# Layer 1's attention on one core: softmax weights turned by a product with diag(1/sum), head outputs added up turned in one PSUM bank, values as the stationary operand

## The chip, the cores and the metric

One core of one Trainium2 chip runs the whole program: nine stages, one after the other, in one launch. The metric is device time in microseconds (us). Three timed runs of the kernel before took 13870.17, 13870.44 and 13876.11 us, median 13870.44. Engines are named as in the profile: PE is TensorE's matmul, PEld its load of a stationary operand ("weights"), DVE is VectorE, ACT is ScalarE, POOL is GpSimd, SP is SyncE.

## The reference, cut to what matters

The program chains a windowed token mixer and four layers of attention and feed-forward over `h`, 32 samples of 242 tokens and 64 channels. The change is within layer 1's attention, `h = h + attn(layernorm(h))`:

```
q = _rmsnorm(_rope(x @ wq.T as 16 heads of 64), q_norm_w)     # per head
k = _rmsnorm(_rope(x @ wk.T), k_norm_w);  v = x @ wv.T         # one key/value head for all 16
mask = (cols <= rows) & (rows - cols <= 128)
scores = where(mask, q @ k.T * 64**-0.5, -1e30)
attn = softmax(scores, axis=-1)
out = (attn @ v, heads side by side) @ wo.T
```

## The kernel before, in words

`stage_l1_attn` handles 32 samples x 16 heads = 512 units `u = b * 16 + n`. The 242 tokens of a sample are two tiles of 121 (`TP`). Because of causality, query tile 0 sees key block 0 and query tile 1 sees key blocks 0 and 1, so a head's scores are three blocks of 121x121, kept side by side in 363 columns.

What is done once for a sample is `prepare(b + 1, ...)`, in twelve named pieces for TensorE: `turn` (x transposed), `q0` to `q3` (queries, only for their sums of squares), `k`, `k_turn`, `fold`, and `v0` to `v3`, which multiply x with `vo`, the product of `wv` and each head's part of `wo`. So `vs[c][:, t, n, :]` holds, for head n, values that already carry the output projection, and a head's outputs only have to be added to the others'. `PE_AT`, `AC_AT` and `DV_AT` (L740 to L743) say behind which head of the sample before each piece is issued on each engine. Heads 0, 7, 8 and 15 carry no piece on TensorE. The square root of `root` (head 8, ScalarE) needs another table than the exponential, so ScalarE loads a table twice for each sample.

Work for a head is spread over four engines' in-order queues, with semaphores between them. The steps, with the number of heads by which each trails `project`:

- `project` (L800, PE, 0): turned queries into PSUM `Y`; `turn_by_rope` (L962, DVE, 0): times the rotation table, to SBUF `y`.
- `score` (L805 and L807, PE, 1): the mask enters PSUM as a bf16 product, then two fp32 products with the keys add to it.
- `peak` (L968, L971, DVE, 1): maxima of rows; `soften` (L889, ACT, 2): exponential, PSUM to `s`.
- `turn` (L795, PE, 3): three transposes of 121x121 blocks; `move` (L895, ACT, 3): PSUM to `pT`.
- `blend` (L816, PE, 4): three products, each with a block of turned weights `pT` as the stationary operand and 65 columns of values moving. `vs` has a 65th column of ones for each head (`V1 = C + 1`), so column 64 of the result is the sum of the weights.
- `collect` (L977, L985 and L987, L993, DVE, 4): inverse of that sum, product with the result, sum over heads in `acc`; once a sample `h += acc`.

Each iteration on TensorE is `turn(u-3)`, `project(u)`, `score(u-1)`, `blend(u-4)`, then a piece of preparation. On VectorE it is `collect(u-4)`, `turn_by_rope(u)`, `peak(u-1)`, then a piece. On ScalarE it is `move(u-3)`, `soften(u-2)`, then a piece. The loops are unrolled in Python: no order is chosen at run time. `load_all` (L147) sets ones and zeros by memsets on VectorE (L159), starts the loads once these are done, and works the layer norm in between. `since(eng, sem, n)` (L753) is a wait that is left out for n <= 0.

Of the kernel before, what the change touches and what calls it, by code (L numbers as in the profile page):

```python
# [11 lines left out]
ALU = mybir.AluOpType  # L12
# [3 lines left out]
B, L, C = 32, 250, 64  # L16
# [660 lines left out]
def stage_l1_attn(nc, h, xn, k, A):  # L677
# [4 lines left out]
    V1 = C + 1  # L682
    two = range(2)
    KEYS, BLOCKS = [slice(0, TP), slice(TP, 3 * TP)], [[0], [1, 2]]
    with ExitStack() as ctx:
# [8 lines left out]
        vs = [sb(f"vs{c}", [TP, NT, NH, V1]) for c in two]  # L694
# [5 lines left out]
        s = [sb(f"s{c}", [TP, 3 * TP]) for c in two]  # L700
        pT = [sb(f"pT{c}", [TP, 3, TP]) for c in two]
        nmax = [sb(f"nmax{c}", [TP, NT]) for c in two]
        den = [sb(f"den{c}", [TP, NT]) for c in two]
        acc = [sb(f"acc{c}", [TP, NT, C]) for c in two]
# [9 lines left out]
            [(vs[c][:, :, :, :], 1.0) for c in two] + [(xT[c][C:128, :], 1.0) for c in two] + [  # L714
# [20 lines left out]
        turned, pT_done, pv_done, inverted, summed, added = sem("turned"), sem("pT_done"), sem("pv_done"), sem("inverted"), sem("summed"), sem("added")  # L735
# [4 lines left out]
        PE, AC, DV = pp.sem[0], pa.sem[0], pd.sem[0]  # L740
        PE_AT = {1: ["turn"], 2: ["q0"], 3: ["q1"], 4: ["q2"], 5: ["q3"], 6: ["k"], 9: ["k_turn"], 10: ["fold"], 11: ["v0"], 12: ["v1"], 13: ["v2"], 14: ["v3"]}
# [9 lines left out]
        def since(eng, sem, n):  # L751
            if not isinstance(n, int) or n > 0:
                eng.wait_ge(sem, n)  # L753

        with nc.Block() as block:
# [6 lines left out]
            def _(pe):  # L762
# [60 lines left out]
                def body(i, begin, last):  # L823
                    for c in two:
                        b = i * 2 + c
                        for n in range(NH):
                            u = b * NH + n
                            ago = lambda d: (u - d, (n - d) % NH, c if n >= d else 1 - c)
                            lead = begin and c == 0
# [5 lines left out]
                            if n == 4:  # L835
                                pe.wait_ge(AC, pa.after(b, "v3"))
                            if not (lead and n < 4):
                                blend(*ago(4))
                            if not (last and c == 1):
                                for name in PE_AT.get(n, ()):  # L840
                                    prepare(b + 1, 1 - c, name)

                def end(u):
                    score(u - 1, NH - 1, 1)
                    for d in range(4):
                        if d < 3:
                            turn(u - 3 + d, NH - 3 + d)
                        blend(u - 4 + d, NH - 4 + d, 1)
# [4 lines left out]
            def _(a):  # L853
# [31 lines left out]
                def soften(u, n, c):  # L885
                    a.wait_ge(nmaxed, u + 1)
                    since(a, turned, u - 1)
                    for t in range(NT):
                        ins = a.activation(s[n % 2][:, KEYS[t]], S[0:TP, n % 2, KEYS[t]], ACT.Exp, bias=nmax[n % 2][:, t:t + 1], scale=rms[c][:, t, n:n + 1])  # L889
                    ins.then_inc(exped, 1)  # L890

                def move(u, n):
                    a.wait_ge(turned, u + 1)
                    since(a, pv_done, u - 1)
                    a.activation(pT[n % 2][:, :, :].rearrange("p b w -> p (b w)"), TR[0:TP, n % 2, 0:3 * TP], ACT.Copy).then_inc(pT_done, 1)  # L895
# [5 lines left out]
                def body(i, begin, last):  # L901
                    for c in two:
                        b = i * 2 + c
                        for n in range(NH):
                            u = b * NH + n
                            ago = lambda d: (u - d, (n - d) % NH, c if n >= d else 1 - c)
                            lead = begin and c == 0
                            if not (lead and n < 3):
                                move(*ago(3)[0:2])
                            if not (lead and n < 2):  # L910
                                soften(*ago(2))
                            if not (last and c == 1):
                                for name in AC_AT.get(n, ()):
                                    prepare(b + 1, 1 - c, name)

                def end(u):
                    for d in range(3):
                        move(u - 3 + d, NH - 3 + d)
                        if d < 2:
                            soften(u - 2 + d, NH - 2 + d, 1)  # L920

# [3 lines left out]
            def _(v):  # L925
# [47 lines left out]
                def collect(u, n, c, b):  # L973
                    at = PV[0:TP, 0:2 * V1].rearrange("p (t c) -> p t c", t=NT)
                    v.wait_ge(pv_done, u + 1)
                    since(v, summed, u - 1)
                    v.reciprocal(den[n % 2][:, :], at[:, :, C]).then_inc(inverted, 1)  # L977
                    v.wait_ge(inverted, u + 1)
                    if n:
                        v.wait_ge(summed, u)  # L980
                    else:
                        since(v, added, b - 1)
                    for t in range(NT):
                        if n == 0:
                            ins = v.tensor_scalar(acc[c][:, t, :], at[:, t, 0:C], den[n % 2][:, t:t + 1], None, ALU.mult)  # L985
                        else:
                            ins = v.scalar_tensor_tensor(out=acc[c][:, t, :], in0=at[:, t, 0:C], scalar=den[n % 2][:, t:t + 1], in1=acc[c][:, t, :],  # L987
                                                         op0=ALU.mult, op1=ALU.add)
                    ins.then_inc(summed, 1)
                    if n == NH - 1:  # L990
                        tiles = bass.ds(b * NT, NT)
                        v.wait_ge(summed, u + 1)
                        v.tensor_tensor(h[:, tiles, :], h[:, tiles, :], acc[c][:, :, :], ALU.add).then_inc(added, 1)  # L993
# [5 lines left out]
                def body(i, begin, last):  # L999
                    for c in two:  # L1000
                        b = i * 2 + c
                        for n in range(NH):
                            u = b * NH + n
                            ago = lambda d: (u - d, (n - d) % NH, c if n >= d else 1 - c)
                            lead = begin and c == 0
                            if not (lead and n < 4):
                                collect(*ago(4), b if n >= 4 else b - 1)
                            turn_by_rope(u, n)
                            if n == 1:
                                v.wait_ge(DV, pd.after(b, "q_scale"))  # L1010
                            if not (lead and n < 1):
                                peak(*ago(1))
                            if not (last and c == 1):
                                for name in DV_AT.get(n, ()):
                                    prepare(b + 1, 1 - c, name)

                def end(u):
                    peak(u - 1, NH - 1, 1)
                    for d in range(4):
                        collect(u - 4 + d, NH - 4 + d, 1, PAIRS * 2 - 1)  # L1020
# [2196 lines left out]
```

## Time and profile before

| | us |
|---|---|
| timed runs, median of 3 | 13870.44 |
| profiled execution, its own time | 13867.26 |
| its span, first to last instruction | 13865.4 |
| layer 1's attention, first projection to the last head's addition | 1478.16 to 2984.87 |

The profile is of one execution. Each busy time is from the first to the last nanosecond of an instruction, and neighbours on an engine overlap, so distances from start to start are what instructions cost in a dense stretch. A timeline row merges equal instructions that follow one another ("x6") and shows in brackets for how long the engine had been idle before and what released it. `121*64` behind a matmul's names would read: 121 rows and 64 columns of the array in use, then the moving operand's shape. Each fp32 product is two records, since it is done in two passes; a transpose and a bf16 product are one. In the profile's names digits are left out: `a_ps` is this stage's `a1_ps`, and other attention stages share these names, so lines tell them apart. TensorE's granted clock is 1.00 through the stage.

### The profile page before, as it was taken

To read this page: it belongs to the slowest core of one execution; us is meant where nothing else is said; L and a number is where in the kernel's file an instruction comes from. 1 tells how busy PE (TensorE), PEld (TensorE's weight loads), DVE (VectorE), ACT (ScalarE), POOL (GpSimd) and SP (SyncE) were. 2 spreads that over 40 slices of the span, in tenths; PEclk is the share of its full clock that TensorE was granted. 3 is DMA by queue.
4 is the path that set the end of the run, shared out by engine and by line. 5 is a ranking of instruction groups with operands and counts; after the bars stand their busy time and mean duration, and the time that the engine had idled before them with its cause. 6 is when DMAs were issued, how large, how long until landed. Compare 5 with 4: busy or idle time off the path is not lost. (4 is left out here: it accounts for less than half of the span.)

```text
span 13865.4 us, 173167 instructions
## 1 busy us (share of the span) xinstructions
PE 9359.3 (68%) x41773; PEld 6063.9 (44%) x41773; DVE 8477.1 (61%) x30632; ACT 5323.7 (38%) x12786; POOL 2229.3 (16%) x2261
## 2 busy tenths in 40 slices
PE   2696899976959999999999999998941010000100
PEld 2585677754844444444444444446931010000000
DVE  7656666656767888888888888876658411111112
ACT  2463466642435555555555555554520000000000
POOL 0000000000000000000000000000000577777774
PEclk6797899987979999999999999998965555555555
DMA  0000000000004333333333333330010342222222
GB/s 5 4 1 2 5 1 1 1 3 2 1 16 99 95 94 98 93 94 97 93 94 98 94 93 98 94 98 18 1 24 0 56 24 21 21 22 21 26 23 38
DMA packets 452719, 614.34 MB, mean 44 GB/s; under 512 B 167338, under 2 KB 420803, under 8 KB 431582
## 3 DMA queue, kind: packets, MB, share of 16 engines
q1 hardware_dynamic: 377058, 564.22, 16.8%
q0 software_dynamic: 74592, 38.28, 4.7%
q8 instruction: 377, 6.18, 0.2%
q14 instruction: 692, 5.67, 0.1%
HBM read 368.03 MB, written 43.76 MB: 30 GB/s over the span
## 5 line engine op out<-in xcount | busy, mean ns | idle before, releaser
L1800 PE MATMUL pm_out<-pm_w,pm_tab 128*128 128x484 f32 x8192 | 4016.1, 571 | 0.5 <-DVE pm_w L2044 0.2
L1905 ACT ACTIVATE pm_e<-pm_sums 128x484 f32<-128x484 f32 x4096 | 2316.1, 573 | 1523.9 <-PE pm_sums L1815 1521.8
L2044 DVE SCALAR_TENSOR_TENSOR pm_w<-pm_sums,pm_e 128x484 f32<-128x484 f32 x4096 | 2655.2, 649 | 145.5 <-ACT pm_e L1905 129.0
L2708 POOL DMA_INDIRECT g_got<-gat_sources,ed_idx x2048 | 1982.8, 968 | 690.8 <-issue 674.5
L1800 PEld LDWEIGHTS pm_out<-pm_w,pm_tab 128*128 128x128 f32 x8192 | 1560.4, 192 | 968.4 <-issue 623.5
L2716 PE MATMUL g_ps<-k_ident,g_xs 121*128 121x121 f32 x32 | 10.6, 435 | 2502.5 <-DVE g_xs L2832 2502.5
L1815 PE MATMUL pm_sums<-pm_mv,pm_pick 96*128 96x484 bf16 x4096 | 1517.3, 371 | 43.7 <-DVE pm_w L2044 23.2
L2845 DVE TENSOR_TENSOR g_e<-g_got,g_b 128x512 f32<-128x512 f32 x16 | 11.1, 692 | 1815.1 <-DMA g_got<-gat_sources,ed_idx 1815.0
L2716 PEld LDWEIGHTS g_ps<-k_ident,g_xs 121*128 121x128 f32 x32 | 5.1, 181 | 2505.5 <-DVE g_xs L2832 2505.5
L113 POOL TENSOR_TENSOR xn<-h,s_st 121x1024 f32<-121x1024 f32 x1 | 2.9, 2940 | 5478.4 <-DVE s_st L94 5478.4
L2777 ACT ACTIVATE g_ex<-g_ex 128x1024 f32<-128x1024 f32 x16 | 16.9, 1056 | 2176.8 <-DVE g_ex L2860 2176.8
L1815 PEld LDWEIGHTS pm_sums<-pm_mv,pm_pick 96*128 96x128 bf16 x4096 | 406.5, 99 | 886.9 <-issue 652.1
L889 ACT ACTIVATE a_s<-a_ps,a_nmax,a_rms 121x121 f32<-121x121 f32 (+1 forms) x1024 | 459.1, 504 | 133.7 <-DVE a_nmax L971 133.3
L1990 DVE MAX8 pm_srt<-pm_sim 121x8 f32<-121x64 f32 x2880 | 472.1, 212 | 5.2
L1937 DVE TENSOR_TENSOR pm_s<-pm_y,pm_mask 121x363 f32<-121x363 f32 x256 | 137.0, 535 | 461.7 <-PE pm_y L1763 461.7
L816 PEld LDWEIGHTS a_pv<-a_vs,a_pT 121*121 121x121 f32 x3072 | 406.5, 186 | 21.3 <-ACT a_pT L895 1.0
L807 PE MATMUL a_ps<-a_kd,a_y 128*121 128x121 f32 (+1 forms) x2048 | 401.7, 318 | 0.0
L977 DVE RECIPROCAL a_den<-a_pv 121x2 f32<-121x2 f32 x512 | 87.1, 170 | 490.0 <-PE a_pv L816 486.6
L816 PE MATMUL a_pv<-a_vs,a_pT 121*121 121x65 f32 x3072 | 385.1, 261 | 0.9 <-DVE a_acc L987 0.9
L1993 DVE MATCH_REPLACE8 pm_sim<-pm_srt,pm_sim 121x64 f32<-121x64 f32 x1920 | 383.2, 207 | 0.0
L2377 PE MATMUL so_ps<-k_ident,so_keys 128*128 128x128 f32 x224 | 50.4, 418 | 487.1 <-DVE so_keys L2407 410.4
L113 POOL TENSOR_TENSOR xn<-h,f_st 121x1024 f32<-121x1024 f32 x2 | 5.9, 2939 | 2178.7 <-DVE f_st L94 2178.7
(560 smaller groups left out, 18568.0 us busy)
## 6 DMA issues: line engine op xcount, KB each, us to landing
pm_tab<-in_L_ffn_tables SPq DMA_DIRECT2D x128, 2048.0 KB, 8.3
pm_mv<-pm_parts SPq DMA_DIRECT2D x3072, 60.5 KB, 2.4
g_got<-gat_sources,ed_idx POOLq DMA_INDIRECT x2048, 2.6
pm_gb<-pk_threshold_rows SPq DMA_DIRECT2D x128, 242.0 KB, 7.8
gat_running<-g_rec SPq DMA_DIRECT2D x16, 1536.0 KB, 5.7
gat_expert_rows<-g_y SPq DMA_DIRECT2D x32, 242.0 KB
g_y<-gat_expert_rows SPq DMA_DIRECT2D x4, 1936.0 KB
gat_heads<-ed_same SPq DMA_DIRECT2D x4, 1024.0 KB
```

What stands on the lines that cost most here:

```text
L807: ins = pe.matmul(S[0:TP, n % 2, KEYS[t]], y[n % 2][:, t * TP:(t + 1) * TP], kd[c][:, 0:(t + 1) * TP], start=False, stop=(t == NT - 1))
L816: ins = pe.matmul(PV[0:TP, at:at + V1], pT[n % 2][:, b, :], vs[c][:, j, n, :], start=(j == 0), stop=(j == t))
L889: ins = a.activation(s[n % 2][:, KEYS[t]], S[0:TP, n % 2, KEYS[t]], ACT.Exp, bias=nmax[n % 2][:, t:t + 1], scale=rms[c][:, t, n:n + 1])
L977: v.reciprocal(den[n % 2][:, :], at[:, :, C]).then_inc(inverted, 1)
L1800: pe.matmul(out[:, hd % 2, 0:CHUNK], tab[hd % 2][:, t, :], w[:, t % NW, :], start=(t == 0), stop=(t == KT - 1)).then_inc(used, 1)
L1815: pe.matmul(sums[:, t % NB, 0:CHUNK], pick[:, t % 2, :], mv[hd % 2][:, t // 2, :], start=True, stop=True).then_inc(sums_ready, 1)
L1905: a.activation(e[:, t % NW, :], sums[:, t % NB, 0:CHUNK], ACT.Exp).then_inc(exp_ready, 1)
L1937: v.tensor_tensor(s[c][:, :], Y[0:TP, 0:3 * TP], mask[:, :], ALU.add).then_inc(step[c], 1)
L1990: ins = v.max(srt[:, n // 2, n % 2, r8:r8 + 8], x)
L1993: ins = v.match_replace(x, srt[:, n // 2, n % 2, r8:r8 + 8], x, NEG)
L2044: v.scalar_tensor_tensor(out=w[:, t % NW, :], in0=sums[:, t % NB, 0:CHUNK], scalar=0.0, in1=e[:, t % NW, :], op0=ALU.is_gt, op1=ALU.mult). ...
L2708: g.indirect_dma_start(got[c][:, w, :], None, rows, bass.IndirectOffsetOnAxis(ap=idx[:, i * W + w:i * W + w + 1].bitcast(U32), axis=0)).th ...
```

## The change

The sum of a row's weights now comes from the exponential itself (`accum_out=den`), and `vs` has 64 columns for each head, without the ones; their two memsets go. VectorE's new `part` inverts the two sums of a row and scales the identity by them (`share`, 121x121 for each query tile). `turn` becomes three fp32 products with a block of weights stationary and `share` moving, which turns and divides at once; it trails by 4 heads. `blend` trails by 5: values are stationary (121 rows, 64 columns), turned weights move (242 and 121 columns), and all 16 heads add up in one bank, in its partitions 0 to 63 for even samples and 64 to 127 for odd ones. Once a sample ScalarE copies this to `oT` (`move_out`), TensorE turns it back (`turn_out`, behind head 3's weights) and VectorE adds it to `h`. VectorE's `collect` for each head is gone.

```diff
-        vs = [sb(f"vs{c}", [TP, NT, NH, V1]) for c in two]
+        vs = [sb(f"vs{c}", [TP, NT, NH, C]) for c in two]
...
-            [(vs[c][:, :, :, :], 1.0) for c in two] + [(xT[c][C:128, :], 1.0) for c in two] + [
+            [(xT[c][C:128, :], 1.0) for c in two] + [
...
+        OUT_HEAD = 3
...
-                def turn(u, n):
-                    pe.wait_ge(exped, u + 1)
+                def turn(u, n, b):
+                    pe.wait_ge(shared, u + 1)
                     since(pe, pT_done, u - 1)
-                    for b in range(3):
-                        ins = pe.transpose(TR[0:TP, n % 2, b * TP:(b + 1) * TP], s[n % 2][:, b * TP:(b + 1) * TP], ident[0:TP, 0:TP])
+                    if n % NH == OUT_HEAD + 2:
+                        since(pe, added, b)
+                    for blk in range(3):
+                        ins = pe.matmul(TR[0:TP, u % 2, blk * TP:(blk + 1) * TP], s[u % 3][:, blk * TP:(blk + 1) * TP], share[u % 2][:, min(blk, 1), :], start=True, stop=True)
+                    if n % NH == OUT_HEAD and b:
+                        turn_out(u, b - 1)
+                        return
+                    ins.then_inc(turned, 1)
+
+                def turn_out(u, b):
+                    pe.wait_ge(out_moved, b + 1)
+                    for t in range(NT):
+                        ins = pe.transpose(TR[0:TP, u % 2, 3 * TP + t * C:3 * TP + (t + 1) * C], oT[b % 2][:, t * TP:(t + 1) * TP], ident[0:C, 0:C])
                     ins.then_inc(turned, 1)
...
-                def blend(u, n, c):
+                def blend(u, n, c, b):
                     pe.wait_ge(pT_done, u + 1)
-                    since(pe, summed, u)
-                    for t in range(NT):
-                        at = t * V1
-                        for j, b in enumerate(BLOCKS[t]):
-                            ins = pe.matmul(PV[0:TP, at:at + V1], pT[n % 2][:, b, :], vs[c][:, j, n, :], start=(j == 0), stop=(j == t))
-                    ins.then_inc(pv_done, 1)
+                    if n == 0:
+                        pe.wait_ge(AC, pa.after(b, "v3"))
+                        since(pe, out_moved, b - 1)
+                    to = slice(C * (b % 2), C * (b % 2) + C)
+                    pe.matmul(PV[to, 0:T], vs[c][:, 0, n, :], pT[u % 2][:, 0:2, :].rearrange("p b w -> p (b w)"), start=(n == 0), stop=False)
+                    pe.matmul(PV[to, TP:T], vs[c][:, 1, n, :], pT[u % 2][:, 2, :], start=False, stop=(n == NH - 1)).then_inc(pv_done, 1)
...
-                            if not (lead and n < 3):
-                                turn(*ago(3)[0:2])
                             project(u, n, c)
+                            if not (lead and n < 4):
+                                turn(*ago(4)[0:2], of(4))
                             if not (lead and n < 1):
                                 score(*ago(1))
-                            if not (lead and n < 4):
-                                blend(*ago(4))
+                            if not (lead and n < 5):
+                                blend(*ago(5), of(5))
...
                 def soften(u, n, c):
                     a.wait_ge(nmaxed, u + 1)
-                    since(a, turned, u - 1)
+                    since(a, turned, u - 2)
                     for t in range(NT):
-                        ins = a.activation(s[n % 2][:, KEYS[t]], S[0:TP, n % 2, KEYS[t]], ACT.Exp, bias=nmax[n % 2][:, t:t + 1], scale=rms[c][:, t, n:n + 1])
+                        ins = a.activation(s[u % 3][:, KEYS[t]], S[0:TP, n % 2, KEYS[t]], ACT.Exp, bias=nmax[n % 2][:, t:t + 1], scale=rms[c][:, t, n:n + 1],
+                                           accum_out=den[u % 3][:, t:t + 1])
...
+                def move_out(b):
+                    a.wait_ge(pv_done, (b + 1) * NH)
+                    if b >= 2:
+                        a.wait_ge(added, b - 1)
+                    a.activation(oT[b % 2][:, :], PV[C * (b % 2):C * (b % 2) + C, 0:T], ACT.Copy).then_inc(out_moved, 1)
...
-                def collect(u, n, c, b):
...
+                def part(u):
+                    v.wait_ge(exped, u + 1)
+                    since(v, inverted, u - 1)
+                    v.reciprocal(den[u % 3][:, :], den[u % 3][:, :]).then_inc(inverted, 1)
+                    since(v, turned, u - 1)
                     v.wait_ge(inverted, u + 1)
...
+                        ins = v.tensor_scalar(share[u % 2][:, t, :], ident[0:TP, 0:TP], den[u % 3][:, t:t + 1], None, ALU.mult)
+                    ins.then_inc(shared, 1)
+
+                def collect(u, b):
+                    v.wait_ge(turned, u + 1)
...
+                    v.tensor_tensor(h[:, tiles, :], h[:, tiles, :], TR[0:TP, u % 2, 3 * TP:3 * TP + NT * C].rearrange("p (t c) -> p t c", t=NT), ALU.add).then_inc(added, 1)
```

On ScalarE `move` trails by 4 and `move_out(b - 1)` follows it at head 5. On VectorE the order is now `turn_by_rope(u)`, `part(u-3)`, `peak(u-1)`, with `collect(u-5, b-1)` behind that at head 8 alone.

## Rows read from the trace of the kernel before

**Rows 1.** Windows: span; busy us (count) of PE, PEld, DVE, ACT, POOL; clock.

```profile
1479.00:2985.00 1506.00, 1429.98 (x8966) 1152.58 (x8964) 972.98 (x3988) 914.46 (x2002) 0.00 (x0) 1.00 0.00 1
```

**Rows 2.** Groups by line and form: busy us, mean ns, idle before, its releaser.

```profile
L977 DVE RECIPROCAL a_den<-a_pv 121x2 f32<-121x2 f32 x512 | 87.1, 170 | 490.0 <-PE a_pv L816 486.6
```

**Rows 3.** Timeline, PE, heads 14 and 15: start us, length, instruction.

```profile
2032.80 0.48 PE L795 MATMUL a_pt<-k_ident,a_s 121*121 121x121 f32 x3
2033.11 0.58 PE L800 MATMUL a_py<-a_xT,a_wq 128*128 128x242 f32 x2
2033.53 0.32 PE L805 MATMUL a_ps<-a_maskb,a_identb 121*121 121x363 bf16 x1
2033.69 0.78 PE L807 MATMUL a_ps<-a_kd,a_y 128*121 128x121 f32 x4
2034.31 0.75 PE L816 MATMUL a_pv<-a_vs,a_pT 121*121 121x65 f32 x6
2034.89 1.07 PE L789 MATMUL a_pp<-a_vo,a_xT 128*121 128x512 f32 x2
2035.80 0.48 PE L795 MATMUL a_pt<-k_ident,a_s 121*121 121x121 f32 x3
...
2037.90 0.53 PE L795 MATMUL a_pt<-k_ident,a_s 121*121 121x121 f32 x3
```

**Rows 4.** Timeline, all engines, one head of the last sample.

```profile
2955.54 0.17 DVE L977 RECIPROCAL a_den<-a_pv 121x2 f32<-121x2 f32 x1 [1.03 <-PE a_pv L816]
...
2956.14 0.40 DVE L962 TENSOR_TENSOR a_y<-a_py,a_rope 128x242 f32<-128x242 f32 x1
...
2956.69 0.34 PE L805 MATMUL a_ps<-a_maskb,a_identb 121*121 121x363 bf16 x1 [0.20 <-DVE a_y L962]
...
2957.48 0.75 PE L816 MATMUL a_pv<-a_vs,a_pT 121*121 121x65 f32 x6
...
2958.27 0.17 DVE L977 RECIPROCAL a_den<-a_pv 121x2 f32<-121x2 f32 x1 [1.03 <-PE a_pv L816]
```

**Rows 5.** Timeline, PE: first projection, the wait behind head 9's keys, last projection.

```profile
1478.16 1.82 PE L800 MATMUL a_py<-a_xT,a_wq 128*128 128x242 f32 x4
...
2020.72 0.58 PE L795 MATMUL a_pt<-k_ident,a_s 121*121 121x121 f32 x3 [0.96 <-ACT a_s L889]
...
2972.28 0.58 PE L800 MATMUL a_py<-a_xT,a_wq 128*128 128x242 f32 x2
```

**Rows 6.** Timeline, PE, in layer 2's feed-forward: a 64-row product between 128-row ones.

```profile
4732.03 0.98 PE L1800 MATMUL pm_out<-pm_w,pm_tab 128*128 128x484 f32 x2
4732.93 0.88 PE L1763 MATMUL pm_y<-pm_kv,pm_q 64*121 64x121 f32 x4
4733.74 0.38 PE L1815 MATMUL pm_sums<-pm_mv,pm_pick 96*128 96x484 bf16 x1
4733.96 0.98 PE L1800 MATMUL pm_out<-pm_w,pm_tab 128*128 128x484 f32 x2
4734.77 0.37 PE L1815 MATMUL pm_sums<-pm_mv,pm_pick 96*128 96x484 bf16 x1
```

**Rows 7.** Timeline, PE, same stage: 64x64, and 121 rows by 8 columns.

```profile
4422.19 0.62 PE L1757 MATMUL pm_x<-pm_xa,pm_wq 64*64 64x242 f32 x2
4422.74 0.38 PE L1815 MATMUL pm_sums<-pm_mv,pm_pick 96*128 96x484 bf16 x1
...
6344.55 0.97 PE L1800 MATMUL pm_out<-pm_w,pm_tab 128*128 128x484 f32 x2
6345.45 0.37 PE L1796 MATMUL pm_out<-k_ident,pm_tg 121*8 121x121 f32 x2
6345.76 0.38 PE L1815 MATMUL pm_sums<-pm_mv,pm_pick 96*128 96x484 bf16 x1
```

**Rows 8.** Layer 2's attention, one source line: ns min/median/max of an accumulator's read.

```profile
L1312 ACT ACTIVATION_READ_ACCUMULATOR a_e<-a_ps,a_nmax x512: 192/198/212, 3406.0 to 3981.7; 121x1 f32 x171
```

**Rows 9.** Groups by line and form, VectorE: memsets of the values; a 128x128 scaling.

```profile
L159 DVE MEMSET a_vs<- 121x2080 f32 x2 | 3.6, 1792 | 1.2 <-PEq L579 0.8 <-issue 0.4
...
L2127 DVE TENSOR_SCALAR a_wf<-a_wf 128x128 f32<-128x128 f32 x1 | 0.2, 227 | 0.7 <-PEq L155 0.7
```

More of the change, by code:

```diff
@@ L681, in stage_l1_attn @@
     EPS = 1.1920929e-07
-    V1 = C + 1
-    two = range(2)
+    two, three = range(2), range(3)
     KEYS, BLOCKS = [slice(0, TP), slice(TP, 3 * TP)], [[0], [1, 2]]
@@ L699, in stage_l1_attn @@
         y = [sb(f"y{c}", [128, T]) for c in two]
-        s = [sb(f"s{c}", [TP, 3 * TP]) for c in two]
+        s = [sb(f"s{c}", [TP, 3 * TP]) for c in three]
         pT = [sb(f"pT{c}", [TP, 3, TP]) for c in two]
         nmax = [sb(f"nmax{c}", [TP, NT]) for c in two]
-        den = [sb(f"den{c}", [TP, NT]) for c in two]
-        acc = [sb(f"acc{c}", [TP, NT, C]) for c in two]
+        den = [sb(f"den{c}", [TP, NT]) for c in three]
+        share = [sb(f"share{c}", [TP, NT, TP]) for c in two]
+        oT = [sb(f"oT{c}", [C, T]) for c in two]
         psum = lambda n, *d: ctx.enter_context(nc.psum_tensor("a1_" + n, [128, *d, BANK], F32))
@@ L734, in stage_l1_attn @@
         y_done, roped, s_done, maxed, nmaxed, exped = sem("y_done"), sem("roped"), sem("s_done"), sem("maxed"), sem("nmaxed"), sem("exped")
[L735 removed]
+        turned, pT_done, pv_done, inverted, shared, out_moved, added = (
+            sem("turned"), sem("pT_done"), sem("pv_done"), sem("inverted"), sem("shared"), sem("out_moved"), sem("added"))
         quarters = [(t, q) for t in range(NT) for q in range(2)]
@@ L844, in end @@
                     score(u - 1, NH - 1, 1)
[L845 to L848, printed above, removed]
+                    for d in range(5):
+                        if d < 4:
+                            turn(u - 4 + d, NH - 4 + d, PAIRS * 2 - 1)
+                        blend(u - 5 + d, NH - 5 + d, 1, PAIRS * 2 - 1)
+                    since(pe, pT_done, u)
+                    turn_out(u, PAIRS * 2 - 1)
                 samples(pe, first, body, end)
@@ L907, in body @@
                             lead = begin and c == 0
-                            if not (lead and n < 3):
-                                move(*ago(3)[0:2])
+                            if not (lead and n < 4):
+                                move(*ago(4)[0:2])
+                            if n == 5 and b:
+                                move_out(b - 1)
                             if not (lead and n < 2):
@@ L916, in end @@
                 def end(u):
-                    for d in range(3):
-                        move(u - 3 + d, NH - 3 + d)
+                    for d in range(4):
+                        move(u - 4 + d, NH - 4 + d)
                         if d < 2:
                             soften(u - 2 + d, NH - 2 + d, 1)
+                    move_out(PAIRS * 2 - 1)
                 samples(a, first, body, end)
@@ L1005, in body @@
                             lead = begin and c == 0
-                            if not (lead and n < 4):
-                                collect(*ago(4), b if n >= 4 else b - 1)
                             turn_by_rope(u, n)
+                            if not (lead and n < 3):
+                                part(u - 3)
                             if n == 1:
@@ L1012, in body @@
                                 peak(*ago(1))
+                            if b and n == OUT_HEAD + 5:
+                                collect(u - 5, b - 1)
                             if not (last and c == 1):
@@ L1018, in end @@
                     peak(u - 1, NH - 1, 1)
-                    for d in range(4):
-                        collect(u - 4 + d, NH - 4 + d, 1, PAIRS * 2 - 1)
+                    for d in range(3):
+                        part(u - 3 + d)
+                    collect(u, PAIRS * 2 - 1)
                 samples(v, first, body, end)
```

26 lines of the change are left out of this document (5 added, 21 removed).

## Prediction, made before the run

> **What bounds the kernel now.** I read the windows of the stage first: from 1479 to 2985 us TensorE is busy for 1430 of 1506 us at full clock, VectorE for 973 and ScalarE for 914 [rows 1]. That makes TensorE the suspect, but its ends are modelled, so I went to the timeline and took distances from start to start. In heads 14 and 15 it is truly full: a head goes transposes 0.31, project 0.42, mask 0.16, scores 0.62, blend 0.58, and a piece of preparation 0.91, which adds up to the 3.00 from one `turn` to the next, and the head without a piece takes 2.10 (2035.80 to 2037.90) [rows 3]. Sixteen heads are 33.6 us; eight pieces q0 to q3 and v0 to v3 are 7.3; the other four pieces are nine short passes, at the passes of rows 3 (0.105 us for 121 columns, 0.205 for 242) some 1.15. So TensorE has 42.0 us of work for a sample. It takes more: from the first projection to the last are 1494.1 us for 511 heads [rows 5], 2.92 each, 46.8 us for a sample. The 4.8 us between are waits, in two places.
>
> The first is a loop through VectorE. In the last sample, without preparation, a head takes 2.73 us, from one reciprocal to the next [rows 4]: 0.60 for reciprocal and two additions to the start of `turn_by_rope`, 0.55 until the mask product starts behind it, 0.79 for mask and scores, 0.79 from blend's first product to the next reciprocal. VectorE's `collect` waits for blend, `turn_by_rope` is queued behind it, and the next `score` waits for that. The groups show it as 487 us of VectorE's idle time before L977, released by blend [rows 2]: idle time of an engine that is not full, but on the loop. The second place is once a sample, behind `k_turn`: the root's table, the exponential's table and the exponentials hold the next `turn` for 0.96 us [rows 5].
>
> **What goes.** `collect` leaves the loop: in the new order VectorE never waits for blend before `turn_by_rope`, and `part` waits for exponentials three heads back. What is late next is TensorE's own work. So the question is what that is now.
>
> **The product instead of the transposes.** Three transposes are three records, 0.31 us. Two fp32 products of `score` are four records: two passes of 121 columns and two of 242 in 0.62 us, 0.105 and 0.205 each [rows 3]. Three products with 121 moving columns are six passes of 0.105, 0.63 us. Added: 0.32 a head. The bounds are 0 (a product costs what the transpose did) and 0.35; rows with the same shapes are so near that I take 0.32.
>
> **Blend.** Now six passes of 65 columns, spaced by the load of 121 columns rather than by their own length: 0.58. After: two passes of 242 and two of 121 columns, 0.41 + 0.20 = 0.61. Added: 0.03. By passes alone a head is 0.42 + 0.63 + 0.16 + 0.62 + 0.61 = 2.44.
>
> **The stationary operand's new shape.** No product of this stage uses less than 121 rows and columns today; blend will use 121x64, between 121x121 ones. The nearest rows lie in layer 2's feed-forward [rows 6, 7]. Two passes of L1800 take 0.81 us when a 96x128 product follows (4733.96 to 4734.77), and 0.90 when the 64x121 product L1763 does (4732.03 to 4732.93): 0.09 on the way in. L1763 itself has exactly the passes of two `score` products, 0.62, and takes 0.81: 0.19 more, of which 0.09 is the way out and 0.10 the load of its first 121 columns, no longer hidden behind a running product. L1757 (64x64, two passes of 242, 0.41) takes 0.55: 0.09 out and 0.05 for its first load of 64 columns. That few columns alone do it, with all rows in use, shows L1796: 121 rows and 8 columns, again 0.90 ahead of it, and its two passes of 121 take 0.31 instead of 0.21 [rows 7]. So each blend pays 0.09 in, 0.05 load, 0.09 out, and whatever follows 0.10 for its own load of 121 or 128 columns: 0.33 us a head. Nothing hides it, since the loop that idled is gone. Below it could be 0 if 64 columns count as the full width, 0.19 if loads stay hidden, above some 0.40. I take 0.33, the sum of rows. A head is then 2.77.
>
> This is where a rule of the Trainium skill speaks against the change: "TensorEngine Tiling (Array Packing)", Key Properties, has it that going from one tiling mode to another drains TensorE. The trace agrees with 0.09 us each way [rows 6]. The skill's "TensorE: Matmul & The Clock Gate", Step-by-step, says that weights are loaded ahead of running products; the trace agrees in a dense stretch (0.105 us from pass to pass) but not across a change of shape. With all loads hidden the sum below would be about 13990, with the exposed loads it is 14054.
>
> **The rest of TensorE's sample.** Pieces q and v: 8 x 0.86, since the 0.05 that each waited for its load is in the 0.33 now; 6.9. Other pieces 1.15. `turn_out` is two transposes of 64 rows, 0.21, plus a change each way and loads, 0.6 in all. At `k_turn` the chain over ScalarE is as long as before, while TensorE's own two heads in front of it grow by 0.67 each: of the 0.96 us I leave 0.25, bounds 0 and 0.96. Together 16 x 2.77 + 6.9 + 1.15 + 0.6 + 0.25 = 53.2 us a sample.
>
> **Other engines.** ScalarE is busy for 914/512 = 1.79 us a head; two reads of the accumulator at 0.20 [rows 8] make it 2.19, against 53.2/16 = 3.3. Hidden; `move_out` is one copy a sample. VectorE is at 1.90; it loses two additions of a head and gains two scalings of 121x121, some 0.22 each by the 128x128 one [rows 9]: no change, hidden. If TensorE were not the bound, both would add to the latency of a head, but with lags of 4 and 5 heads they have one head's time more.
>
> **The sum.** 511 heads at 53.2/16 are 1699; the last sample has no pieces and no wait, -8; the first four heads issue no `turn` and the first five no `blend`, 7 us of work, of which I count 5, the rest being first latencies. 1686 us, against 1494: +192. Ahead of the stage two memsets go, 3.6 us and their gap of 0.4, on VectorE's path to the layer norm [rows 9]: -4. Behind the last head, products and copies in a row take the place of others: -1, between -3 and +2. Together +187 on the profiled execution's 13867.26 us: 14054. The median of the timed runs is 3 us higher, which is nothing here.
>
> **Rivals.**
> The narrow operand is free (8%). Rows 7 speak against it: L1796 is narrow in columns alone and pays. If 64 columns count as the whole width, a head is 2.44; with turn_out at 0.2 and 0.85 left of the wait behind `k_turn`, a sample is 48.1, between projections 1523 us; minus 5 that is 13892, hardly slower than now.
> ScalarE's chain once a sample lengthens (8%). The two reads of the accumulator lie in it, and `part` behind them. If the wait behind `k_turn` grows to 1.5 us instead of shrinking to 0.25, that is 39 us more: 14093. For it speaks that the wait is there today; against it, that TensorE arrives later.
> Faster: the freed loop is worth more than the work added (4%). In place is the 2.73 us of a head without pieces, which could fall towards TensorE's own work. It decides if a head costs TensorE less than (46.8 - 8.05 - 0.2 - 0.9)/16 = 2.35 us. If the product costs what the transposes cost and the shape is free, a head is 2.13, a sample 43.3, and the time 13737. Against it: two records for each fp32 product wherever I look [rows 3, 6], which alone puts a head at 2.44.
>
> **How the numbers follow.** The forecast has 80%. Its own range goes from 13980 (loads hidden) to 14110 (0.40 a head for the shape, a longer wait). The ScalarE case ends within it, so 13975 to 14110 leaves out about 2 in 10. A difference under 0.2% (28 us) is what a measurement of this kernel can't tell from none. Slower: 80%, 8% and a good third of the 8% whose centre lies 25 us above: 91%. Same 5%, faster 4%.
>
> **What would show it.** In the profile after: `turn` as six records at 0.105 from start to start (right for the product); L805's idle time released by `turn_by_rope` gone (right for the loop); blend's first record starting 0.30 us behind the last score pass instead of 0.20, and the next instruction's first product 0.20 behind blend's last pass of 121 columns instead of 0.10, with its second pass 0.10 late (right for the shape); heads without a piece at 2.77 us, heads with q or v at 3.63. Wrong would be: a head without a piece near 2.44 (shape free), TensorE idle in front of `turn` in every head released by `part` (another loop took the place), or a granted clock under 1.00 in the stage.

## The result, and the profile after

| | before | after |
|---|---|---|
| median, us | 13870.31 (4 runs, 13869.67 to 13876.11) | 14046.51 (4 runs, 14044.44 to 14049.83) |
| span of the profiled execution | 13865.4 | 14048.0 |
| first to last projection, 511 heads | 1494.1 | 1683.8 |
| a sample, sum of its 16 medians | 46.94 | 53.14 |

The ratio is 1.0125, 95% interval 1.0109 to 1.0140: slower by 176 us, where +187 was forecast. "First to last projection" (called the stage's length below) is the difference of two starts on TensorE, in the kernel after of these two rows ([rows 5] before):

```profile
1478.41 1.82 PE L813 MATMUL a_py<-a_xT,a_wq 128*128 128x242 f32 x4
...
3162.21 0.68 PE L813 MATMUL a_py<-a_xT,a_wq 128*128 128x242 f32 x2
```

The stage is 189.7 us longer by the records of all projections (1686 us were forecast for it, 1683.8 came). The window of the stage (columns as in [rows 1]) now shows a TensorE without idle time, at the same full clock:

```profile
1478.38:3162.19 1683.81, 1682.90 (x9476) 1216.41 (x9474) 989.20 (x3967) 1019.83 (x3041) 0.00 (x0) 1.00 0.00 1
```

Where the time of a head goes is read from start to start. This is one head of the last sample, which carries no piece of preparation, and the start of the next:

```profile
3119.25 0.62 PE L829 MATMUL a_pv<-a_pT,a_vs 121*64 121x242 f32 x2
3119.71 0.37 PE L830 MATMUL a_pv<-a_pT,a_vs 121*64 121x121 f32 x2
3120.01 0.68 PE L813 MATMUL a_py<-a_xT,a_wq 128*128 128x242 f32 x2
3120.52 0.80 PE L799 MATMUL a_pt<-a_share,a_s 121*121 121x121 f32 x6
3121.16 0.32 PE L818 MATMUL a_ps<-a_maskb,a_identb 121*121 121x363 bf16 x1
3121.31 0.79 PE L820 MATMUL a_ps<-a_kd,a_y 128*121 128x121 f32 x4
3122.03 0.62 PE L829 MATMUL a_pv<-a_pT,a_vs 121*64 121x242 f32 x2
```

Blend 0.76, project 0.51, turn 0.64, mask 0.15, scores 0.72: 2.78 us, forecast 2.77. A head with a piece (here v, L791) takes 3.63, as forecast: 0.96 for the piece, and project is back at 0.41, since the piece now takes over the load that waits:

```profile
2103.00 1.12 PE L791 MATMUL a_pp<-a_vo,a_xT 128*121 128x512 f32 x2
2103.96 0.57 PE L813 MATMUL a_py<-a_xT,a_wq 128*128 128x242 f32 x2
2104.37 0.80 PE L799 MATMUL a_pt<-a_share,a_s 121*121 121x121 f32 x6
```

The loop of [rows 4] is gone. VectorE's timeline of the same head of the last sample: `turn_by_rope` (L986) starts 0.72 us behind the first record of its projection (3120.01), as soon as its second pass is done, and nothing of blend stands ahead of it:

```profile
3120.73 0.41 DVE L986 TENSOR_TENSOR a_y<-a_py,a_rope 128x242 f32<-128x242 f32 x1 [0.57 <-PE a_py L813]
3121.05 0.16 DVE L1000 RECIPROCAL a_den<-a_den 121x2 f32<-121x2 f32 x1
3121.32 0.67 DVE L1004 TENSOR_SCALAR a_share<-k_ident,a_den 121x121 f32<-121x121 f32 x2
```

The groups by line and form (columns as in [rows 2]) give the new operations their means: a share 281 ns (0.22 was taken from [rows 9]), a read of the accumulator 203 ns (L903; [rows 8] had 198). The idle time that was 487 us behind blend is now 286 behind the projection, and it is on no one's path.

```profile
L1004 DVE TENSOR_SCALAR a_share<-k_ident,a_den 121x121 f32<-121x121 f32 x1022 | 243.3, 281 | 56.9 <-DVE a_den L1000 1.9 <-PE a_pt L799 0.5
L986 DVE TENSOR_TENSOR a_y<-a_py,a_rope 128x242 f32<-128x242 f32 x512 | 207.9, 406 | 285.6 <-PE a_py L813 285.6
L829 PEld LDWEIGHTS a_pv<-a_pT,a_vs 121*64 121x64 f32 x1018 | 97.5, 135 | 159.1 <-ACT a_pT L910 158.5 <-issue 0.3
```

The last line names a suspect that the prediction had not: TensorE's load path stands idle 158.5 us in all in front of blend's load, and the profile lays it on ScalarE's copy to `pT`. Either the array's narrow shape costs these microseconds, or a late copy does. The experiments had to tell that apart, and to split 0.67 us a head into the product and the shape. The trace of the kernel after speaks on the first by itself: taken in order, the copy that a blend needs has ended 3.82 us (median of 512) before that blend's first load starts.

### The profile page after: what moved, and what is told of

The parts are those of the page before. It is cut to its first block and busy times, and to the rows that moved or that the text cites. A ratio compares the mean times of both kernels' runs of the same rounds, so it can differ in the third digit from the quotient of the medians.

```text
span 14048.0 us, 174954 instructions
## 1 busy us (share of the span) xinstructions
PE 9623.7 (69%) x42349; PEld 6143.3 (44%) x42349; DVE 8497.0 (60%) x30630; ACT 5430.7 (39%) x13842; POOL 2230.0 (16%) x2261
## 5 line engine op out<-in xcount | busy, mean ns | idle before, releaser
L2799 ACT ACTIVATE g_ex<-g_ex 128x1024 f32<-128x1024 f32 x16 | 16.9, 1056 | 2186.0 <-DVE g_ex L2882 2186.0
L903 ACT ACTIVATE a_s<-a_ps,a_nmax,a_rms 121x121 f32<-121x121 f32 (+1 forms) x1024 | 502.4, 500 | 0.8
L799 PEld LDWEIGHTS a_pt<-a_share,a_s 121*121 121x121 f32 x3072 | 401.2, 186 | 31.8 <-DVE a_share L1004 11.0
L799 PE MATMUL a_pt<-a_share,a_s 121*121 121x121 f32 x3072 | 413.4, 270 | 0.5 <-DVE a_share L1004 0.3
L992 DVE TENSOR_REDUCE a_nmax<-a_ps 121x1 f32<-121x121 f32 (+1 forms) x1024 | 305.7, 340 | 127.4 <-PE a_ps L820 114.6
```

Of the source, the lines that this page charges most:

```text
L799: ins = pe.matmul(TR[0:TP, u % 2, blk * TP:(blk + 1) * TP], s[u % 3][:, blk * TP:(blk + 1) * TP], share[u % 2][:, min(blk, 1), :], start=T ...
L903: ins = a.activation(s[u % 3][:, KEYS[t]], S[0:TP, n % 2, KEYS[t]], ACT.Exp, bias=nmax[n % 2][:, t:t + 1], scale=rms[c][:, t, n:n + 1], ac ...
L992: ins = v.tensor_reduce(nmax[n % 2][:, t:t + 1], S[0:TP, n % 2, KEYS[t]], AX.X, ALU.max, negate=True)
```

## The experiments

The first four and the last three of these runs were made on one chip, late_collect, paired and late_keys on another. The kernel before took 14079.49 us beside the first four, 13873.97 beside the middle three, and 14076.38 beside the last three. Profiles put the 200 us outside this stage (wide128 needs 11105.6 us from its last projection to the end of its span, the kernel after 10885.8), so kernels are compared by their ratio to the kernel before on the same chip and by the stage's length.

**wide128: the kernel after, with a full-width stationary operand in blend.** Blend loads 128 columns of `vs`, the head's 64 and those of the next, whose results land in partitions that nobody reads.

```diff
-                    pe.matmul(PV[to, 0:T], vs[c][:, 0, n, :], ...
+                    pe.matmul(PV[0:wide, 0:T], vs[c][:, 0, n * C:n * C + wide], ...   # wide = 128
```

> The changed kernel, but blend loads 128 columns of values (the head's 64 and the next head's 64, whose results in partitions 64 to 127 nobody reads) and both samples' sums use partitions 0 to 63, so move_out comes before blend's first product of the next sample. Theory (change of the array's shape, 0.33 us a head): blend's first pass follows the last score pass by 0.20 instead of 0.30 us, a head without a piece takes 2.45 instead of 2.78 us, a sample 48.5 instead of 53.1 us; 13898 us. Rival (blend really waits for ScalarE's copy of the turned weights, as the 158 us of idle load time put down to pT say): the wait stays, 14030 to 14050 us.

Ratio 1.0029 (1.0018 to 1.0041); stage 1542.0 us, a head 2.45, a sample 48.66. Loading twice the columns makes the head 0.33 us shorter. The copy to `pT` has less time here, since the head is shorter, and yet the wait on it is gone. In the waits (engine and line waited for: us, times, longest), the kernel after has this line:

```profile
PEld a_pv L829 <- ACT a_pT L910: 158.5, 506, 0.3
```

In wide128 L829 has no line among TensorE's waits; in paired (below), with half as many changes of shape, it has half:

```profile
PEld a_pv L829 <- ACT a_pT L912: 79.4, 253, 0.3
```

So what the profile lays on ScalarE is the change of shape. Which half of the partitions the narrow result goes to plays no part: in the kernel after, a head without a piece takes 2.78 us in even samples (partitions 0 to 63) and in odd ones (64 to 127).

**wide65: the same with 65 columns.** One line differs (`wide = 65`).

> As wide128, with 65 columns loaded instead of 128. Theory (the array changes shape only when the stationary operand has 64 columns or fewer): as wide128, within 10 us, 13890 us. Rival (any operand narrower than its neighbours pays): 14040 us.

Ratio 1.0025 (1.0015 to 1.0035), stage 1538.1, a head 2.45. The timeline shows where the 0.33 went: from scores to blend 0.62 instead of 0.72, blend 0.62 instead of 0.76, project 0.42 instead of 0.51.

```profile
3005.44 0.79 PE L820 MATMUL a_ps<-a_kd,a_y 128*121 128x121 f32 x4
3006.06 0.57 PE L829 MATMUL a_pv<-a_pT,a_vs 121*65 121x242 f32 x2
3006.47 0.37 PE L830 MATMUL a_pv<-a_pT,a_vs 121*65 121x121 f32 x2
3006.68 0.58 PE L813 MATMUL a_py<-a_xT,a_wq 128*128 128x242 f32 x2
3007.10 0.80 PE L799 MATMUL a_pt<-a_share,a_s 121*121 121x121 f32 x6
```

One column more than 64 is as good as 128: between 64 and 65 lies a step of 0.33 us a head.

**scale_turn: the kernel after, with transposes in place of the product.** VectorE scales the weights themselves (121 and 242 columns) instead of the identity.

```diff
-                        ins = pe.matmul(TR[...], s[u % 3][...], share[u % 2][:, min(blk, 1), :], start=True, stop=True)
+                        ins = pe.transpose(TR[...], s[u % 3][...], ident[0:TP, 0:TP])
-                        ins = v.tensor_scalar(share[u % 2][:, t, :], ident[0:TP, 0:TP], den[...], None, ALU.mult)
+                        ins = v.tensor_scalar(s[u % 3][:, KEYS[t]], s[u % 3][:, KEYS[t]], den[...], None, ALU.mult)
```

> The changed kernel, but VectorE scales the weights themselves by the inverse sums (121 and 242 columns) and TensorE turns them by three transposes instead of the products; blend stays at 64 columns. Theory (the product's second pass costs 0.32 us a head on TensorE, which is the bound): a head without a piece 2.46 us, 14046 - 0.32 x 511 + 8 for a longer wait behind k_turn = 13891 us. Rival (the loop over part decides, since the transposes now wait for scaled weights): TensorE idle ahead of turn, 13950 us or more.

Ratio 1.0028 (1.0017 to 1.0040), stage 1542.1, a head 2.46: three transposes take 0.32 us and three products 0.64. The product costs 0.32.

**scale_turn_wide: both.**

> Both edits together. Theory (the two costs add, and the freed loop then pays): a head without a piece 2.13 us, a sample 43.4 us, 13735 us, faster than the kernel before. Rival (a loop of latencies takes over below 2.4 us a head): 13800 to 13870 us.

Ratio 0.9928 (0.9912 to 0.9945), stage 1400.1, a head 2.14, a sample 44.21 rather than 43.4. Heads 9 and 10 take 3.14 and 3.31, 0.79 and 0.76 above their own passes (2.14 and the piece). Of head 9's, 0.37 is there in the last sample too (2.51 against 2.14), where no keys are prepared: that part is another wait, shown below at blend_first. The rest is the wait behind the root's chain. The two costs add up: 1683.8 minus 141.8 or 141.7 for either, and 283.7 for both.

**late_collect: the kernel before, with one edit, `collect` behind `turn_by_rope` on VectorE.** It takes VectorE's wait for blend out of the loop and changes nothing else.

```diff
-                            if not (lead and n < 4):
-                                collect(*ago(4), b if n >= 4 else b - 1)
                             turn_by_rope(u, n)
+                            if not (lead and n < 4):
+                                collect(*ago(4), b if n >= 4 else b - 1)
```

> The kernel before with one edit: on VectorE collect(u-4) stands behind turn_by_rope(u) instead of ahead of it. Theory (the loop blend, collect, turn_by_rope, score held heads without a piece at 2.73 us and hid TensorE's slack of 4.8 us a sample): a head without a piece 2.10 to 2.15 us, a sample 43.5 us instead of 46.9, first to last projection 1387 instead of 1494 us, ratio to the kernel before 0.992. Rival (another wait, such as blend for the addition of the head before, takes over at once): ratio 0.998 to 1.000.

Ratio 0.9965 (0.9952 to 0.9977), stage 1450.8: 43 us less, where 107 were expected. That was a miss. Every second head still takes 2.62, the others 2.15; the timeline shows why:

```profile
2913.16 0.75 PE L816 MATMUL a_pv<-a_vs,a_pT 121*121 121x65 f32 x6
2914.17 0.58 PE L795 MATMUL a_pt<-k_ident,a_s 121*121 121x121 f32 x3 [0.26 <-ACT a_s L889]
```

Here `turn` starts 1.01 us behind blend's first record, in the next head 0.59: three heads behind its projection it meets exponentials that are not ready. The loop was not one wait but two, and the second came up once the first was gone.

**paired: the kernel after, blends of two heads together behind every second.** As many narrow products, half as many changes of shape.

```diff
-                            if not (lead and n < 5):
-                                blend(*ago(5), of(5))
+                            if n % 2:
+                                for d in (6, 5):
+                                    if not (lead and n < d):
+                                        blend(*ago(d), of(d))
```
(four `pT` buffers instead of two, `move_out` at head 6.)

> The changed kernel with the blends of two heads issued one after the other behind every second head (four buffers pT, move_out one head later); all products and shapes stay. Theory (0.33 us is paid for each change of shape and back, not for each narrow product): half of it goes, 0.165 us a head, first to last projection 1600 instead of 1684 us. Rival (each product with 64 columns costs that much by itself): 1680 us.

Ratio 1.0066 (1.0049 to 1.0083), stage 1601.1. Without a piece two heads take 1.92 + 3.29 = 5.21 instead of 5.56. So 0.35 is saved for one change of shape there and back left out: the price is of the change, not of the narrow product. In an ordinary pair the two blends follow one another, 1.38 us for both:

```profile
3065.21 0.62 PE L829 MATMUL a_pv<-a_pT,a_vs 121*64 121x242 f32 x2
3065.67 0.37 PE L830 MATMUL a_pv<-a_pT,a_vs 121*64 121x121 f32 x2
3065.88 0.57 PE L829 MATMUL a_pv<-a_pT,a_vs 121*64 121x242 f32 x2
3066.28 0.37 PE L830 MATMUL a_pv<-a_pT,a_vs 121*64 121x121 f32 x2
3066.59 0.68 PE L813 MATMUL a_py<-a_xT,a_wq 128*128 128x242 f32 x2
```

One pair in each sample is different, the one at head 5, of the last head of a sample and the first of the next:

```profile
3053.88 0.64 PE L829 MATMUL a_pv<-a_pT,a_vs 121*64 121x242 f32 x4
3054.34 0.39 PE L830 MATMUL a_pv<-a_pT,a_vs 121*64 121x121 f32 x4
3054.66 0.68 PE L813 MATMUL a_py<-a_xT,a_wq 128*128 128x242 f32 x2
```

Its results go to different halves of the partitions (0 to 63 and 64 to 127), and its two blends run side by side: their first records start 0.013 us apart in all 31 samples (0.67 in every other pair), and both take 0.78 us together, where one alone takes 0.76. That is 0.6 us a sample. Against it, head 9 takes 4.30 in the last sample instead of 3.29, by the wait shown at blend_first. So the 82.7 us by which the stage is shorter are a sum of such terms, and 82.7 / 256 = 0.32 is no measurement of one change; the 0.35 of an ordinary pair is.

**late_keys: scale_turn_wide, `k_turn` to `v3` one head later.** It gives the root's chain a head more.

```diff
-    9: ["k_turn"], 10: ["fold"], 11: ["v0"], 12: ["v1"], 13: ["v2"], 14: ["v3"]
+    10: ["k_turn"], 11: ["fold"], 12: ["v0"], 13: ["v1"], 14: ["v2"], 15: ["v3"]
```

> scale_turn_wide (weights scaled by VectorE, three transposes, 128 columns loaded) with the pieces k_turn, fold and v0 to v3 and what belongs to them on the other engines one head later. Theory (what is left over TensorE's own work, 1.6 us a sample, is the chain over the root's table behind heads 8 to 10, half of it k_turn waiting for the scaled keys): 0.6 us a sample goes, first to last projection 1381 instead of 1400 us, ratio to the kernel before 0.991. Rival (the wait moves on to the exponentials behind the second table load): 1400 us.

Ratio 0.9925 (0.9908 to 0.9941), stage 1406.6: no gain. Head 9 falls to 2.51, but head 10, which now carries `k_turn`, takes 3.73. The waits show what `turn` waits for there, the scaled weights, in 32 samples 1.5 us at most:

```profile
PEld a_pt L798 <- DVE a_s L1002: 35.7, 32, 1.5
```

The wait was moved, not removed: `k_turn` no longer waits, but `turn` in head 10 does. The 2.51 of head 9 is what it takes in the last sample as well. The rival had put the wait behind ScalarE's second table. The timeline (first two rows VectorE, last TensorE) shows it behind the first, on VectorE: `inv` (L970) stands idle for the root, and the scaling that `turn` needs (L1002) is queued behind it. The exponentials behind the second table start at 2388.03, too late to be what VectorE had waited for.

```profile
2386.39 0.37 DVE L970 RECIPROCAL a_rms<-a_rms 121x34 f32<-121x34 f32 x1 [1.24 <-ACT a_rms L887]
...
2387.82 0.54 DVE L1002 TENSOR_SCALAR a_s<-a_s,a_den 121x121 f32<-121x121 f32 x2
...
2388.41 0.58 PE L798 MATMUL a_pt<-k_ident,a_s 121*121 121x121 f32 x3 [0.75 <-DVE a_s L1002]
```

**blend_first: the kernel after, blend ahead of scores.** It makes a bf16 product follow the narrow one, to see what the follower's load is worth.

```diff
-                            if not (lead and n < 1):
-                                score(*ago(1))
                             if not (lead and n < 5):
                                 blend(*ago(5), of(5))
+                            if not (lead and n < 1):
+                                score(*ago(1))
```

> The changed kernel with blend ahead of score instead of behind it, so that the bf16 mask product follows the narrow products and not an fp32 one; nothing else. Theory (0.33 us are two drains of 0.09 and two loads that nothing covers, 0.05 for 64 fp32 columns and 0.10 for 121 or 128; a bf16 load of 121 columns behind a change of shape shows 0.01 in the kernel before): 0.09 us a head goes, a head without a piece 2.69, first to last projection 1638 instead of 1684 us. Rival (all of what follows the narrow products is drain): 1684 us.

Ratio 1.0119 (1.0102 to 1.0136), stage 1677.8. The head is 2.72, near what was expected (2.69): the mask takes 0.20 instead of 0.15, so a bf16 load of 121 columns shows 0.05, half of an fp32 load's 0.10.

```profile
3122.92 0.62 PE L829 MATMUL a_pv<-a_pT,a_vs 121*64 121x242 f32 x2
3123.38 0.37 PE L830 MATMUL a_pv<-a_pT,a_vs 121*64 121x121 f32 x2
3123.68 0.37 PE L818 MATMUL a_ps<-a_maskb,a_identb 121*121 121x363 bf16 x1
3123.88 0.79 PE L820 MATMUL a_ps<-a_kd,a_y 128*121 128x121 f32 x4
```

But the stage gained 6 us and not 46, and a sample fell by 0.19 only: head 9 grew from 3.09 to 3.94. The root's chain is not the cause, since head 9 takes 3.73 in the last sample too (2.83 in the kernel after), where nothing is prepared. The trace shows the cause there:

```profile
3133.94 0.29 DVE L1012 TENSOR_TENSOR h<-h,a_pt 121x128 f32<-121x128 f32 x1
...
3134.37 0.86 PE L799 MATMUL a_pt<-a_share,a_s 121*121 121x121 f32 x6 [0.78 <-DVE h L1012]
```

`turn` at head 9 waits until VectorE has added the last sample's output to `h`, since that output lies in the PSUM buffer that `turn` is to write next (`since(pe, added, b)` in the diff). On VectorE the addition is queued at head 8 behind `peak`, which waits for the scores, and these now come later. The wait is the new dataflow's own, and the prediction had no term for it: by the last sample it costs head 9 only 0.05 us in the kernel after, but 0.37 in scale_turn_wide and 1.01 here and in paired.

**deep_before: the arithmetic of before in the schedule of after.** Transposes, sums by the 65th column and VectorE's `collect` stay; `project` comes first, `turn` trails by 4, `blend` and `collect` by 5, `collect` stands behind `turn_by_rope`, `s` has three buffers.

```diff
-                            if not (lead and n < 3):
-                                turn(*ago(3)[0:2])
                             project(u, n, c)
+                            if not (lead and n < 4):
+                                turn(*ago(4)[0:2])
...
-                            if not (lead and n < 4):
-                                blend(*ago(4))
+                            if not (lead and n < 5):
+                                blend(*ago(5))
```

> The kernel before (transposes, weights stationary, 65 moving columns, no change of shape) with the changed kernel's schedule: project first, turn 4 heads back, blend and collect 5 heads back, three buffers s, collect behind turn_by_rope. Theory (late_collect gave only 43 of 107 us because turn, 3 heads back, then waited for its exponentials in every second head): a head without a piece 2.13, a sample 43.9 us, first to last projection 1393 instead of 1494 us. Rival (collect's wait for blend on VectorE keeps a loop): 1440 to 1455 us as in late_collect.

Ratio 0.9919 (0.9902 to 0.9935), stage 1383.2 (1393 expected): the shortest stage of all, with 110.9 us gone and not one product changed.

```profile
2861.40 0.63 PE L800 MATMUL a_py<-a_xT,a_wq 128*128 128x242 f32 x2
2861.86 0.48 PE L795 MATMUL a_pt<-k_ident,a_s 121*121 121x121 f32 x3
2862.18 0.32 PE L805 MATMUL a_ps<-a_maskb,a_identb 121*121 121x363 bf16 x1
2862.33 0.79 PE L807 MATMUL a_ps<-a_kd,a_y 128*121 128x121 f32 x4
2862.96 0.75 PE L816 MATMUL a_pv<-a_vs,a_pT 121*121 121x65 f32 x6
2863.54 0.63 PE L800 MATMUL a_py<-a_xT,a_wq 128*128 128x242 f32 x2
```

**scale_turn_wide_again: scale_turn_wide once more, beside deep_before.**

> The same kernel as scale_turn_wide, beside deep_before on one chip: ratio to the kernel before 0.993, as deep_before's within 0.1%.

Ratio 0.9922 (0.9906 to 0.9939), stage 1400.1 again. By the whole time it can't be told from deep_before; by the stage it is 16.9 us longer.

## Why the prediction was right

The change is a sum of three things with different signs, and the runs give each (stage's length, us):

| step | kernel | length | difference |
|---|---|---|---|
| before | before | 1494.1 | |
| the schedule alone | deep_before | 1383.2 | -110.9 |
| new dataflow, transposes, 128 columns | scale_turn_wide | 1400.1 | +16.9 |
| product with the inverse sums | wide128 | 1542.0 | +141.9 |
| 64 columns instead of 128 | after | 1683.8 | +141.8 |

Of the 16.9 us, `turn_out` is some 15 (head 7 takes 0.48 more than its neighbours in each of 31 samples); the rest is a balance of waits.

- **The loop.** The prediction had 4.8 us of waits in a sample and let all but 0.25 go. In the last sample heads fell from 2.73 to TensorE's own work, in deep_before to 2.14 against the 2.10 counted in [rows 3]. Right, though the path was longer than described: late_collect shows that moving `collect` alone frees less than half, and deep_before that the rest of the schedule (`turn` a head later and behind `project`, a third buffer `s`) frees what is left. Which of these parts does it is not separated.
- **The product.** +0.32 a head forecast, 0.31 to 0.32 measured (2.45 against 2.14 and 2.78 against 2.46). Six records of 0.105, as named.
- **The shape.** +0.33 a head forecast from an unrelated stage's rows; 0.32 to 0.33 measured, with its parts: in front of blend 0.09 to 0.10, within and behind it 0.14 of 0.14 forecast, the follower's load 0.10. paired shows that it is paid for each change. The rule of the Trainium skill that stood beside this step, "TensorEngine Tiling (Array Packing)", Key Properties, gives a drain and no price; the 0.09 us each way fit it, and the loads that are no longer hidden are nearly half of the price.
- **Over the stage each of these is 0.28 us a head, not 0.32.** The waits in heads 9 and 10 shrink as TensorE gets slower, and give some of it back: with the product these two heads take 3.15 and 3.31 (wide128), without it 3.14 and 3.31 (scale_turn_wide).
- **The wait behind `k_turn`.** 0.25 a sample forecast. Now 3.09 for head 9 and 3.46 for head 10, together 0.3 to 0.4 above their work, 0.05 of it the wait for the addition to `h`. It is spread over two heads and small records, as here in head 10, where project takes 0.53 instead of 0.41, turn 0.74 instead of 0.63 and mask 0.20:

```profile
2089.61 0.58 PE L813 MATMUL a_py<-a_xT,a_wq 128*128 128x242 f32 x2
2090.14 0.90 PE L799 MATMUL a_pt<-a_share,a_s 121*121 121x121 f32 x6
2090.88 0.37 PE L818 MATMUL a_ps<-a_maskb,a_identb 121*121 121x363 bf16 x1
2091.08 0.79 PE L820 MATMUL a_ps<-a_kd,a_y 128*121 128x121 f32 x4
```

- **`turn_out`.** 0.6 forecast, 0.49 measured: head 7 of the last sample takes 3.27 against 2.78. By luck this error and that of the wait cancel within a sample: 53.2 forecast, 53.14 came.
- **The memsets, -4.** They are gone, but the first projection starts where it did (1478.41 against 1478.16). VectorE's timelines before (first fence) and after (second) show that the stage ahead, whose code is the same, ended 4.7 us later in this execution. From the start of that stage's last addition to the first projection are 64.94 or 64.95 us in the three kernels with the two memsets (before, late_collect, deep_before) and 60.48 or 60.49 in the four without any memset of `vs` (after, scale_turn, paired, blend_first). So the forecast saving is real, 4.5 us, and scatter ahead of it hid it.

```profile
1412.61 0.89 DVE L674 TENSOR_TENSOR h<-h,f_y 121x128 f32 x4
1414.29 1.79 DVE L159 MEMSET a_vs<- 121x2080 f32 x1 [0.79 <-PEq L579]
```

```profile
1417.32 0.89 DVE L674 TENSOR_TENSOR h<-h,f_y 121x128 f32 x4
1418.61 0.52 DVE L159 MEMSET a_xT<- 64x242 f32 x2 [0.40 <-PEq L579]
```

- **Behind the last head, -1 forecast.** From the last projection to the end of the last addition were 12.59 us and are 12.15.
- **The rest of the error.** 189.7 in the stage, +0.3 ahead, -0.4 behind the last head and -6.9 in the stages behind, whose code is the same, make the 182.6 by which the spans differ. The prediction had no term for the last one, and no run explains it: on one chip, seven profiled runs with the same code behind this stage took from 11073.0 to 11093.5 us there. The medians differ by 176. The total can't test the prediction more finely than that; 1686 against 1683.8 us of the stage can.

The rivals: the free narrow operand is out by wide65; ScalarE's longer chain is out, as the wait behind `k_turn` shrank; "faster" had the right mechanism and the wrong side of its own break-even of 2.35 us a head. scale_turn_wide, at 2.14, shows the other side of it: 0.7% faster. The prediction had put 13737 on that case. scale_turn_wide's stage is 94.0 us shorter than before, not 125: in heads 9 and 10 1.5 us of waits remain where the rival had left 0.9, and `turn_out` costs 0.48 where it had 0.2. (The rival's own terms, 16 x 2.13 + 8.05 + 0.2 + 0.9, add up to 43.2, not to its 43.4.)

## What to carry to other kernels

Price the shape of a stationary operand, not only its passes: here 64 columns between wider ones cost 0.33 us for each round trip, and one column more cost nothing, so widen it with columns that no one reads, or issue narrow products together. Two narrow products whose results go to different halves of the partitions ran side by side in paired; a kernel that gives neighbouring heads different halves could save 0.6 us a pair more, an estimate from 1.38 against 0.78 that no run tests. Count every fp32 product that replaces a transpose as twice the transpose's records (0.64 against 0.32 us for three). When an edit brings a new schedule and a new arithmetic, run the old arithmetic in the new schedule: here that was the gain, and the rest had eaten it. Look at the last sample when a wait is to be blamed on preparation: it has none, and a wait that is still there has another cause.

## What the hardware showed that was not expected

- The step lies exactly between 64 and 65 columns of the stationary operand: 2.78 and 2.45 us a head with the same rows, moving columns and number of passes.
- The load that a change of shape exposes depends on type and width: 0.10 us for 121 or 128 fp32 columns, 0.05 for 64 fp32 and for 121 bf16 columns. The rows of before had suggested 0.01 for the bf16 one ([rows 6]: L1815 takes 0.215 us behind the narrow L1763 and 0.207 behind wide products). That operand has 96 rows and 128 columns, not 121 and 121; no run shows which of these makes the difference.
- The profile lays the cost of the shape on whoever signalled last: 158.5 us of idle load "released" by ScalarE's copy, in front of blend. With 128 columns the line is gone, and with half the changes it is halved. An idle time that comes 506 times with much the same length (0.31 us in the mean, 0.3 at most) is the sign of a cost in the engine itself.
- Two products with 64 columns each, whose results go to partitions 0 to 63 and 64 to 127, ran at the same time (starts 0.013 us apart in 31 of 31 samples of paired, 0.78 us for both blends), without the kernel asking for it.
